# The node-wise programs between two edge passes of a graph network, each joined into one block

## What is computed

```python
# end of layer 1: softmax-weighted sum over the edges, then
out = elu(agg) + feat @ W_res
x = layernorm(x + out)
# layer 2
h = x @ w_in + b_in
for l in range(2):
    xn = layernorm(h) * ln1_g[l] + ln1_b[l]
    q, k, v = xn @ wq[l] + bq[l], xn @ wk[l] + bk[l], xn @ wv[l] + bv[l]
    ...            # attention over the edges (and each node with itself) gives agg
    h = h + agg @ wo[l] + bo[l]
    xn2 = layernorm(h) * ln2_g[l] + ln2_b[l]
    h = h + gelu(xn2 @ w1[l] + b1[l]) @ w2[l] + b2[l]     # w1: 256x1024, w2: 1024x256
x = layernorm(x + h)
# layer 3
all_h = einsum('ni,rio->nro', x, weight)                  # eight relations
msg = all_h[src, rel]
...
```

## Time and profile before

| what | us |
|---|---|
| three runs, median (lowest to highest) | 5597.12 (5595.05 to 5604.28) |
| span of the profiled execution | 5598.0 |
| stage A, 2352.2 to 2556.5 of the span | 204.3 |
| stage B, 3283.3 to 3660.2 | 376.9 |
| stage C, 4390.5 to 4901.4 | 510.9 |

### The profile page before, as it was taken

The page is one execution under the profiler, slowest core; times in us unless marked ns, Lnnn a source line. Parts: engine busy times, 40 slices in busy tenths (PEclk is TensorE's granted clock), DMA queues, the critical chain, the costliest instruction groups (busy, mean ns, idle before and its releaser), DMA issues. The chain is left out here.

```text
span 5598.0 us, 59687 instructions
## 1 busy us (share of the span) xinstructions
PE 3837.7 (69%) x16239; PEld 2931.1 (52%) x16239; DVE 3567.2 (64%) x6753; ACT 1691.0 (30%) x3460; POOL 2922.7 (52%) x2898
## 2 busy tenths in 40 slices
PE   1666577774887888656777758877777496955551
PEld 0565266662446677434555538655555384444441
DVE  8998655556775777667888862478888622132226
ACT  0001622222772222124555523345554232200000
POOL 3686677776776777304666600056666000077771
PEclk9756766666996777778999979989999798977775
DMA  1243244452113555426777730167777302333333
GB/s 46 55 99 69 44 134 133 130 120 49 18 9 106 137 136 136 84 81 189 203 200 201 193 85 16 64 202 200 199 200 190 84 1 75 145 107 106 105 104 45
DMA packets 280732, 629.94 MB, mean 113 GB/s; under 512 B 70604, under 2 KB 125232, under 8 KB 277296
## 3 DMA queue, kind: packets, MB, share of 16 engines
q0 software_dynamic: 159168, 436.21, 31.2%
q1 hardware_dynamic: 121328, 190.89, 10.6%
HBM read 560.35 MB, written 65.91 MB: 112 GB/s over the span
## 5 line engine op out<-in xcount | busy, mean ns | idle before, releaser
L1001 PE MATMUL edge_sums<-edge_rows,edge_hot 128*128 128x272 f32 (+2 forms) x3712 | 1277.6, 511 | 694.7 <-issue 254.0
L934 POOL DMA_INDIRECT edge_rows<-kv_rows,dst_index x928 | 878.3, 946 | 1160.4 <-POOLq L89 417.9
L1001 PEld LDWEIGHTS edge_sums<-edge_rows,edge_hot 128*128 128x128 f32 x3712 | 939.2, 261 | 964.2 <-issue 337.2
L934 POOL DMA_INDIRECT edge_rows<-rel_rows,dst_other_index x464 | 438.8, 946 | 694.8 <-ACTq L89 553.8
L934 POOL DMA_INDIRECT begun_rows<-xl_rows,dst_index x464 | 450.8, 971 | 193.2 <-issue 130.7
L934 POOL DMA_INDIRECT edge_rows<-rows,src_index x464 | 438.9, 946 | 164.1 <-issue 131.6
L203 POOL DMA_INDIRECT table_src<-src_src_stage_all x333 | 414.4, 1244 | 155.2 <-issue 100.1
L1270 PE MATMUL edge_own_rows<-dst_x,edge_hot_t 128*128 x1856 | 457.2, 391 | 37.7 <-ACT edge_hot_t L965 22.6
L1011 DVE TENSOR_TENSOR l_acc<-l_acc,edge_sums 128x258 f32 (+1 forms) x464 | 197.8, 426 | 396.5 <-PE edge_sums L1001 383.9
L1270 PEld LDWEIGHTS edge_own_rows<-dst_x,edge_hot_t 128*128 128x128 f32 x1856 | 351.2, 194 | 106.1 <-issue 53.5
L1011 DVE TENSOR_TENSOR last_acc<-last_acc,edge_sums 128x256 f32 x232 | 97.7, 421 | 429.8 <-PE edge_sums L1001 429.5
(11 more groups left out here) (436 smaller groups left out, 6552.0 us busy)
## 6 DMA issues: line engine op xcount, KB each, us to landing
edge_where<-local_dst SPq DMA_DIRECT2D x174, 256.0 KB, 3.5
dst_rank_keys<-in_dst SPq DMA_DIRECT2D x85, 312.5 KB, 3.4
rel_rows<-proj_out SPq DMA_DIRECT2D x25, 1024.0 KB, 3.8
edge_where<-local_src SPq DMA_DIRECT2D x58, 256.0 KB, 3.4
edge_rows<-kv_rows,dst_index POOLq DMA_INDIRECT x928, 3.8
kv_rows<-proj_out SPq DMA_DIRECT2D x50, 260.0 KB, 2.0
edge_rows<-rows,src_index POOLq DMA_INDIRECT x464, 2.8
begun_rows<-xl_rows,dst_index POOLq DMA_INDIRECT x464, 2.8
```

Of the source, the lines that this page charges most:

```text
L934: pool.indirect_dma_start(out=self.rows[:, h * U + b, 0:self.width], out_offset=None, in_=self.source[:, :], in_offset=bass.IndirectOffset ...
L1001: last = nc.tensor.matmul(sums[p % len(sums)][:, 0:width], self.hot[s % 2][:, 2 * (p % 4) + i, :], self.half(s)[:, 2 * (p % 4) + i, first: ...
```

## The change

`attend_update` for layer 1, `move`, all of `project`, `Affine`, `feed_forward`, `self_merge` and `norm_into` in the three stages are replaced by three calls of `node_stage`. Each is one block, written out in full (no loops), of 40 slots q = 0 to 39. A slot does on each engine the work of up to three parts, each for another tile:

- part a (`a_at`): merge and add, two tiles in slots 0 and 1 of each five, one in slot 2, none in slots 3 and 4, for q below 25;
- part c (`c_at`): tile q-5, for q from 5 to 29: the `w_in` product, or in B and C the two-layer network (its second half, `lower`, and `add_in` one slot later);
- part e (`e_at`): tile q-15, for q from 15 to 39: the q, k, v product, or in C the eight relations.

Row statistics become scale and shift for five tiles at a time (`spread`, `root`, `finish`), twice per tile group. What was done over 6400 columns is done per tile. Banks: one for each of the transposed c tile, the transposed a or e tile and the lowered product, one for the `wo` product, two raised halves, two for the products of part e. The x rows that part a needs come from DRAM in groups of five tiles; biases before the adds (`base`, `offset`, and the kept x in C) go to POOL; VectorE instead of ScalarE moves the transposed tiles of parts c and e out of PSUM; the small memset after each tile's `post` goes.

```diff
--- before.py
+++ after.py
+class RowNorm:
...
+    def spread(self, nc, dve, step, g):
+        of = slice(g * SLOTS, (g + 1) * SLOTS)
+        st, mean, var, tmp = self.stats[:, of, :], self.mean[:, of], self.var[:, of], self.tmp[:, of]
+        dve.wait_ge(self.measured, (g + 1) * SLOTS)
+        nc.vector.tensor_tensor(mean, st[:, :, 1], st[:, :, 4], ALU.add)
+        nc.vector.tensor_tensor(tmp, st[:, :, 1], st[:, :, 4], ALU.subtract)
+        step(nc.vector.tensor_tensor(var, st[:, :, 2], st[:, :, 5], ALU.add))
+        nc.vector.tensor_scalar(mean, mean, 0.5, None, ALU.mult)
+        nc.vector.scalar_tensor_tensor(tmp, tmp, 0.25, tmp, ALU.mult, ALU.mult)
+        step(nc.vector.tensor_scalar(var, var, 1.0 / C, EPS, ALU.mult, ALU.add))
+        nc.vector.tensor_tensor(var, var, tmp, ALU.add).then_inc(self.varied, 1)
...
+def node_stage(nc, k, tag, x, a, c, e):
...
+    ring = 4
+    last_slot = NT - 1 + 15
+    def a_at(q):
+        g, u = divmod(q, SLOTS)
+        if not 0 <= q < NT:
+            return []
+        return [g * SLOTS + n for n in ((0, 1), (2, 3), (4,), (), ())[u]]
+    def c_at(q):
+        return q - 5 if 5 <= q < NT + 5 else None
+    def e_at(q):
+        return q - 15 if 15 <= q < NT + 15 else None
+    def before_slot(q, at):
+        return sum(1 for n in range(q) if at(n) is not None)
...
+            @block.gpsimd
+            def _(pool):
+                def base(t):
+                    pool.wait_ge(have_x[t // SLOTS], 16)
+                    nc.gpsimd.tensor_tensor(x[:, t, :], x[:, t, :], ba[:, :], ALU.add).then_inc(based, 1)
+                def offset(t):
+                    pool.wait_ge(copied_c, t + 1)
+                    ins = nc.gpsimd.tensor_tensor(x[:, t, :], x[:, t, :], bc[:, :], ALU.add)
+                    if qkv:
+                        ins.then_inc(biased, 1)
+                        return
+                    ins.then_inc(ready, 1)
+                    pool.wait_ge(ready, 1 + t + 1)
+                    pool.wait_ge(have_before[t // SLOTS], 16)
+                    nc.gpsimd.tensor_tensor(x[:, t, :], x[:, t, :], before[:, t % (2 * SLOTS), :], ALU.add).then_inc(biased, 1)
...
+            def bend(t, half):
+                act.wait_ge(raised, 2 * t + half + 1)
+                after(act, lowered, t - 1)
+                for f in range(half * H, (half + 1) * H):
+                    ins = nc.scalar.activation(inner[t % 2][:, f, :], up[half][:, f % H, :], ACT.Gelu, bias=b1[:, f:f + 1])
+                ins.then_inc(bent, 1)
...
+            def multiply_out(t, n):
+                pe.wait_ge(moved_e, t + 1)
+                if qkv:
+                    after(pe, left_v, t * nch + n + 1 - 2)
+                elif n % 2:
+                    after(pe, left_v, t * nch // 2 + n // 2)
+                else:
+                    after(pe, left_a, t * nch // 2 + n // 2)
+                at, m = chunks[n]
+                for h in range(2):
+                    ins = nc.tensor.matmul(prod_e[n % 2][:, 0:m], turned_e[t % ring][:, h, :], we[:, h, at:at + m],
+                                           start=(h == 0), stop=(h == 1))
+                ins.then_inc(multiplied_e, 1)
...
+                if t is not None:
+                    turn_in(t)
+                if t_e is not None:
+                    turn_out(q, t_e)
+                if dense and c_at(q - 1) is not None:
+                    lower(c_at(q - 1))
+                if t is not None:
+                    raise_half(t, 0) if dense else multiply_in(t)
+                if own_merge and mine:
+                    turn_sum(q, mine[0])
+                if t_e is not None:
+                    for n in range(nch // 2 if not qkv else 1):
+                        multiply_out(t_e, n)
+                if dense and t is not None:
+                    raise_half(t, 1)
+                if own_merge and mine:
+                    multiply_sum(mine[0])
+                    for n in mine[1:]:
+                        turn_sum(q, n)
+                if t_e is not None:
+                    for n in range(nch // 2 if not qkv else 1, nch):
+                        multiply_out(t_e, n)
+                if own_merge:
+                    for n in mine[1:]:
+                        multiply_sum(n)
...
+            def merge_own(t):
+                dve.wait_ge(have_rows[t // SLOTS], 16)
+                after(dve, turned_1, t - ring + 1)
+                v = rows[:, t % (2 * SLOTS), :].rearrange("p (h e) -> p h e", e=33)[:, :, 0:32]
+                mine = agg[t % ring][:, :].rearrange("p (h d) -> p h d", d=32)
+                wide = lambda n: both[:, n, t, :].unsqueeze(2).to_broadcast([P, 8, 32])
+                nc.vector.tensor_tensor(mine, sums[:, t, :, 0:32], wide(0), ALU.mult)
+                step(nc.vector.tensor_tensor(v, v, wide(1), ALU.mult))
+                nc.vector.tensor_tensor(mine, mine, v, ALU.add).then_inc(merged, 1)
+            def add_own(t):
+                dve.wait_ge(multiplied_a, t + 1)
+                dve.wait_ge(based, t + 1)
+                nc.vector.tensor_tensor(x[:, t, :], x[:, t, :], prod_a[:, 0:C], ALU.add).then_inc(added_a, 1)
+            def merge_update(t):
+                mine = hp[t % ring][:, :].rearrange("p (h d) -> p h d", d=32)
+                body = every[:, t, :, 0:32]
+                step(nc.vector.tensor_tensor(mine, body, every[:, t, :, 32:33].to_broadcast([P, 8, 32]), ALU.mult))
+                nc.vector.tensor_scalar(body, mine, 0.0, None, ALU.min).then_inc(merged, 1)
+            def add_update(t):
+                dve.wait_ge(moved_a, t + 1)
+                dve.wait_ge(have_rows[t // SLOTS], 16)
+                mine = hp[t % ring][:, :].rearrange("p (h d) -> p h d", d=32)
+                step(nc.vector.scalar_tensor_tensor(mine, mine, 0.0, every[:, t, :, 0:32], ALU.max, ALU.add))
+                step(nc.vector.scalar_tensor_tensor(hp[t % ring][:, :], hp[t % ring][:, :], -1.0, rows[:, t % (2 * SLOTS), :],
+                                                    ALU.add, ALU.add))
+                nc.vector.tensor_tensor(x[:, t, :], x[:, t, :], hp[t % ring][:, :], ALU.add).then_inc(added_a, 1)
+            def move_in(t):
+                dve.wait_ge(turned_2, t + 1)
+                if dense:
+                    after(dve, raised, (t - ring + 1) * 2)
+                    for h in range(2):
+                        ins = nc.vector.tensor_scalar(turned_c[t % ring][:, h, :], turn_c[:, h * P:(h + 1) * P], gain_c[:, h:h + 1],
+                                                      bias_c[:, h:h + 1], ALU.mult, ALU.add)
+                else:
+                    after(dve, lowered, t - ring + 1)
+                    ins = nc.vector.tensor_copy(turned_c[t % ring][:, :, :].rearrange("p c n -> p (c n)"), turn_c[:, 0:C])
+                ins.then_inc(moved_c, 1)
+            def add_in(t):
                 dve.wait_ge(lowered, t + 1)
+                if dense:
+                    dve.wait_ge(biased, t + 1)
+                    nc.vector.tensor_tensor(x[:, t, :], x[:, t, :], down[:, 0:C], ALU.add).then_inc(added_c, 1)
+                else:
+                    dve.wait_ge(saved[t % 5], 16 * (t // 5 + 1))
+                    nc.vector.tensor_tensor(x[:, t, :], down[:, 0:C], bc[:, :], ALU.add).then_inc(added_c, 1)
+            def move_out(t):
+                dve.wait_ge(turned_3, t + 1)
+                after(dve, multiplied_e, (t - ring + 1) * nch)
+                if qkv:
+                    for h in range(2):
+                        ins = nc.vector.tensor_scalar(turned_e[t % ring][:, h, :], turn_x[:, h * P:(h + 1) * P], gain_e[:, h:h + 1],
+                                                      bias_e[:, h:h + 1], ALU.mult, ALU.add)
+                else:
+                    ins = nc.vector.tensor_copy(turned_e[t % ring][:, :, :].rearrange("p c n -> p (c n)"), turn_x[:, 0:C])
+                ins.then_inc(moved_e, 1)
...
+            def post(t):
+                into, q = out[t % OUTS], x[:, t, :]
+                dve.wait_ge(left_v, nch * (t + 1))
+                dve.wait_ge(saved[t // SLOTS] if dense else have_x[t // SLOTS], 16)
+                step(nc.vector.tensor_scalar(q, into[:, 0:C], 32 ** -0.5, None, ALU.mult))
+                step(nc.vector.tensor_tensor(tmp[:, :], q, into[:, C:2 * C], ALU.mult))
+                nc.vector.tensor_reduce(e.self_score[:, t, :], tmp[:, :].rearrange("p (h d) -> p h d", h=8), AX.X,
+                                        ALU.add).then_inc(posted, 1)
+            begin_own() if own_merge else begin_update()
+            if qkv:
+                for n in range(OUTS):
+                    nc.vector.memset(out[n][:, :], 0.0).then_inc(padded, 1)
+                dve.wait_ge(padded, OUTS)
+            for q in range(last_slot + 1):
+                g, u = divmod(q, SLOTS)
+                t, t_e, mine, t_1 = c_at(q), e_at(q), a_at(q), c_at(q - 1)
+                if q == 5:
+                    dve.wait_ge(have_c, have["c"])
```

(58 more changed lines are left out.)

549 lines of the change are left out of this document (323 added, 226 removed).

## The result

| | median, us (lowest to highest) |
|---|---|
| before, 4 runs beside the changed kernel | 5596.09 (5594.97 to 5604.28) |
| after, 4 runs | 5621.66 (5618.17 to 5624.96) |
| ratio after/before, 95% interval | 1.0044 [1.0032, 1.0056] |

The account below looks back on a forecast made before the run. A was taken as bound by DVE and the seams, B and C by PE plus its waits for elementwise programs. 5598.0 + 41 (A) - 24 (B) - 72 (C) = 5543 of span, so 5542 us, range 5500 to 5595.

Parts of the forecast that it names:

- Stage A, DVE's work: Stage A: DVE's operations, normalisations and memsets, gaps included, sum to 185 us, where DVE had 141 before.
- DVE over 180 us busy: Sign that the prediction is right: in a longer stage A, about 245 us, DVE is busy over 180 us.
- The tail's wait: A's ten last slots, part e alone: DVE waits 2.15 us per slot for PE's product at full clock.
- the waits of 2.2 and 3.0: Stage A: DVE's waits per slot with and without part c, in us, at a PE clock of 0.76.
- the 252 of the sum: Stage A's total in us at clock 0.76: 185 + 15 x 2.2 + 10 x 3.0 + 4; 245 was then taken.
- the wait is 1.35 us in a slot with part c: Stage A: DVE's wait for part e's product, with part c's 0.8 us of work between; 1.35 us at full clock.
- the moves cost "27": Stage A: moves out of PSUM, ScalarE's before, add 27 us to DVE's work.
- waits for DVE ... 4: Stage B, slots 15 to 24: PE's waits for DVE add 4 us to 11.1 x 10, making 115.
- Short waits: Rival, chance 0.20: PE keeps full clock in the tails, DVE's small operations overlap more; -93, 5504 us.
- DVE and POOL hold each other up: Rival, chance 0.15: POOL's 125 adds delay DVE instructions, part e's waits are 0.5 longer; +40, 5582 us.
- The clock falls in the network too: Rival, chance 0.10: PE slows in slots 5 to 14 of B and C and C's tail; 5640 us given.
- It doesn't overlap: Rival, chance 0.05: engines work in turn; B and C's 30 full slots cost 1.5 us more each, 5587 us.

Follow-up runs that it names:

- Experiment 2: Changed kernel with two alternating PSUM banks instead of one for part c's product in A: 5589.81 us, ratio 0.9991 to the kernel before.
- experiments 3 and 7: Changed kernel with idle PE products added in A: 5604.36 us; the same plus two banks for part c's product: 6408.63 us on a slower chip.
- experiment 5: Changed kernel with part e's transpose and move out of PSUM one slot earlier in all stages: 6389.36 us on a slower chip, ratio 0.9935 to the kernel before.
- experiment 12: Changed kernel with only A's moves of transposed tiles out of PSUM put back on ScalarE: 5579.37 us (one run).
- Experiment 6: Changed kernel with B's first `wo` add in a slot placed before DVE's second read of part e: 6446.63 us on a slower chip (one run).
- experiment 4: Changed kernel with POOL's adds in B and C replaced by one-column memsets: 5614.93 us (one run).
- experiment 8: Changed kernel with two banks in A, part e one slot ahead and the early `wo` add: 6349.99 us on a slower chip, ratio 0.9864 to the kernel before.

## Why the prediction was wrong, and where it was right

**Stage A, DVE's work: right.** 185 us with gaps were forecast, 182 measured (289.2 less the 107 of waits). The sign "DVE over 180 us busy" still failed, since the busy time leaves out the gaps: 169.7. The tail's wait (2.15 at full clock) was measured at 2.08, and its ten slots with the end took 67.0 us against 64, though with a wait of 2.65 on average instead of 3.0. The clock of slots 15 to 24 and 30 to 39 was 0.76 and 0.83 against 0.76. In the sum the waits of 2.2 and 3.0 stretch the whole product of 2.75 us by the clock, where by the prediction's own account only the first 1.8 us of it are waited for (1.9 and 2.7), and the 252 of the sum was taken down to 245 by judgement.

**Stage A, "the wait is 1.35 us in a slot with part c": wrong, and the step that failed.** It had part e's product start when its tile was moved. In the slots with part c the product of part c stands ahead of it on PE's list, and that waits for a bank which DVE frees after its merges, `move_in` and `move_out`. Measured: 4.2 us on average in such a slot (62.8 in fifteen, 33 in the sum), and 11.5 us per slot from 15 to 24, where the prediction's terms give 6.6 + 14/25 + 2.2 = 9.4. DVE's waits came to 107 instead of 63: 30 of the 44 more are this term, 17 are the waits for part c's transposed tile and before the second read, and the tail has 3.5 less. Against the forecast of A that is a miss of 44 too, but the equal numbers are partly chance, since the forecast was not the sum. The number of banks was known (the account of the change lists one for the lowered product), but the prediction never asked when the turn of the add that frees it comes on DVE's list. Experiment 2 shows the bank (-33, all but 4 us of it in slots 15 to 29), experiments 3 and 7 the clock (-17). Experiments 5 and 12 show that A also pays for the order, but mostly in the slots 30 to 39, where the prediction had it.

**Stage A, the sense of it: right but too mild.** The prediction said that A gets longer since DVE gets more to do. That the moves cost "27" was their length; with their place in the chain they cost 41.5 (experiment 12).

**Stage B: the step that failed is "waits for DVE ... 4".** Slots 15 to 24 took 130.2 us where 115 were forecast. The second `wo` product waits 2.4 to 2.8 us for the add of the first in each of the four slots there with two of them, and PE lost speed behind it. Experiment 6 moves that add forward, and these slots take 115.0. The rest was near: the head and slots 5 to 14 together took 127.4 (123), slots 25 to 29 51.2 (51), the last `lower`, part e alone and the end 69.9 (64.5). Without POOL's adds (experiment 4) B is 6.3 shorter, 2.9 of it in slots 15 to 24.

**Stage C: right within about 10%.** -64.7 against -72, and so in its pieces: the head 32 (32), slots 5 to 14 91 (88), 15 to 24 161 (156), 25 to 29 72 (72), the rest 90 (91). The seams are gone as described. The second `wo` product waits for the add here too, but 1.2 us only, and no experiment changed that order in C. The step ahead (experiment 5) takes 11 more.

**The rivals.** *Short waits*: nothing of it came. *DVE and POOL hold each other up*: part of it exists (6 us in B), not its size. *The clock falls in the network too* was the one case on the slower side, and its total came near, but not its mechanism: the granted clock of B's slots 5 to 14 was 0.97, far from the 0.80 from which it was to decide. The result is slower for another reason, a wait that none of the rivals named. *It doesn't overlap* was given 0.05 and only for the full slots of B and C; in A, where the prediction did not put it, it is the nearest description of what happened. The 0.83 for faster rested on A being well priced, and its one unproven term, the wait in a slot, was let vary only through the clock.

**What the change is worth.** Of the changed kernel's three blocks the one of C gains 65 us, the one of B loses 2, the one of A loses 85. With the two banks, the early add, the step ahead and ScalarE's moves they take 185, 336 and 435 us, together 135 us under the kernel before.

## What to carry to other kernels

When programs are joined into one block with each engine's order written out, list for every PSUM bank who frees it, and where that instruction stands on its engine's list; with one bank per product the writer is tied to that place, and everything behind the writer too. Price a slot by walking its chain through the engines in list order, not by adding the engines' work. The engine with the most work in such a block should not also hold the small moves between two products: here they cost more than their length (41.5 us for 24 us of work).

## What the runs showed of the hardware that was not expected

- **One kernel, 15% apart on different chips.** The kernel before took 5595 and 5600 us on two chips and 6440 and 6439 on two others, with none of the difference in the node stages; each edge pass of layer 2 took 921 to 929 us instead of some 727. In the middle of an edge pass (the kernel before on a chip of the first kind, the kernel of experiment 8 on one of the second, same code there) the granted clock and the DMA rate differ; POOL's gather instructions last 946 and 945 ns on both:

```profile
2700.00:3200.00 500.00, 381.01 (x1533) 291.07 (x1533) 435.43 (x693) 260.92 (x587) 316.68 (x335) 0.93 0.72 201
```

```profile
3100.00:3700.00 600.00, 395.24 (x1421) 296.80 (x1419) 406.94 (x644) 239.00 (x535) 297.41 (x315) 0.79 0.56 157
```

  Which comes first, slower transfers or a lower clock, was not tried. The node stages were equal to within 1.5 us.
- **POOL's adds of 256 columns take 0.73 us in the median** (0.72 to 1.02), and DVE operations with both inputs in SBUF that run beside them take mostly 0.83 to 0.98 us instead of 0.42; the cost in the stage is 6 us of 379.
- **Products that compute nothing can shorten a stage** (-17 us in A, with the clock at 0.80 instead of 0.74), and lengthen it where PE has few holes (+4.5 us).
